# Moving the scaling of half of the value weights from ScalarE to GpSimd at the start of a fused attention and feed-forward block

## What is computed

```
x = x + attn(layernorm(x), Wq, bq, Wk, bk, Wv, bv, Wbeta, bbeta, Walpha, balpha)
x = x + ffn(layernorm(x), gate/up/down weights as 4-bit codes with scales)

attn:  q = (x @ Wq + bq);  k = (x @ Wk + bk);  v = (x @ Wv + bv)
       k = k / norm(k);  alpha = sigmoid(x @ Walpha + balpha);  beta = softplus(x @ Wbeta + bbeta)
       chunks of 128 tokens, 4 heads of 128, decay from cumsum(log(alpha)), state from chunk to chunk
```

## Time and profile before

| what | value |
|---|---|
| median of 3 runs | 1118.35 us (1118.31 to 1118.68) |
| the profiled execution, its own time | 1118.82 us |
| its span in the profile | 1117.1 us |
| TensorE busy | 1106.8 us (99%) |
| VectorE busy | 864.5 us (77%) |
| GpSimd busy | 652.0 us (58%) |
| ScalarE busy | 504.9 us (45%) |

### The profile page before, as it was taken

One profiled execution on the slowest core, in us unless ns is written; L12 is line 12 of the kernel. 1 busy time (PEld: TensorE's weight loads), 2 busy tenths in 40 slices (PEclk: granted clock), 3 DMA queues, 4 the chain that ended last, 5 costly groups with the idle time before them and its releaser, 6 DMA issues.

```text
span 1117.1 us, 22523 instructions
## 1 busy us (share of the span) xinstructions
PE 1106.8 (99%) x8898; PEld 861.3 (77%) x8898; DVE 864.5 (77%) x1516; ACT 504.9 (45%) x1170; POOL 652.0 (58%) x665
## 2 busy tenths in 40 slices
PE   9999999999999899999999999999999999999999
PEld 5656655566457677788888888888888888888886
DVE  7788767468777766688988898889888888886664
ACT  4432345365244344444554455445444544454432
POOL 3376545236783856656775677567756775676330
PEclk9999999999999999999999999999999999999999
DMA  8021111000112223222323232323232323221222
GB/s 305 7 69 47 38 35 42 10 10 1 50 46 76 87 94 114 94 105 104 114 96 106 103 114 95 123 87 114 99 138 78 114 103 123 99 110 77 77 76 76
DMA packets 30233, 96.66 MB, mean 87 GB/s; under 512 B 3440, under 2 KB 3760, under 8 KB 23472
## 3 DMA queue, kind: packets, MB, share of 16 engines
q1 hardware_dynamic: 30128, 95.23, 23.9%
HBM read 63.73 MB, written 31.49 MB: 85 GB/s over the span
## 4 chain that ended last, share of the span: by engine, by line
PE 90%; DVE 3%; POOL 3%; issue 2%; ACT 1%; DMA 0%; SPq 0%; DVEq 0%; POOLq 0%; ACTq 0%
PE ps L649 44%; PE ps L718 19%; PE ps L466 9%; PE ps L758 7%; PE ps L610 6%; PE ps L432 1%; PE ps L552 1%; PE ps L541 1%; PE ps L562 1%; PE ps L476 1%; PE ps L532 0%; PE ps L554 0%; POOL WR L1760 0%; DMA WR<-wqkv 0%; ACT L938 0%
## 5 line engine op out<-in xcount | busy, mean ns | idle before, releaser
L649 PE MATMUL ps<-XT,WR 128*128 128x256 f16 x1344 | 183.3, 273 | 0.0
L649 PE MATMUL ps<-REG,WR 128*128 128x256 f16 x1344 | 183.3, 273 | 0.0
L1059 ACT COPY load<-ps 128x256 f32<-128x256 f32 x168 | 62.4, 371 | 225.7 <-PE ps L649 225.3
L649 PEld LDWEIGHTS ps<-REG,WR 128*128 128x128 f16 x1344 | 130.0, 98 | 21.0
L649 PEld LDWEIGHTS ps<-XT,WR 128*128 128x128 f16 x1344 | 131.5, 98 | 15.4
L1059 ACT COPY bigB<-ps 128x256 f32<-128x256 f32 x168 | 62.5, 372 | 129.5 <-PE ps L649 129.5
L1385 DVE SCALAR_TENSOR_TENSOR X<-ps,X 128x512 f32<-128x512 f32 x161 | 108.0, 683 | 16.2 <-PE ps L718 13.8
L1682 POOL TENSOR_TENSOR ihl_s<-fw,ihl_s 128x512 f16<-128x512 f32 (+1 forms) x46 | 49.5, 1088 | 116.7 <-ACT ihl_s L962 116.7
L1457 DVE TENSOR_TENSOR bigB<-bigB,ps 128x256 f32<-128x256 f32 x168 | 69.5, 414 | 60.2 <-ACT bigB L1059 38.5
L1457 DVE TENSOR_TENSOR load<-load,ps 128x256 f32<-128x256 f32 x168 | 68.7, 413 | 45.3 <-ACT load L1059 31.9
L649 PE MATMUL ps<-REG,bigA 128*128 128x256 f16 x672 | 91.7, 273 | 1.0 <-ACT bigB L1059 1.0
(11 more groups left out here) (244 smaller groups left out, 2536.3 us busy)
## 6 DMA issues: line engine op xcount, KB each, us to landing
kept<-X SPq DMA_DIRECT2D x26, 1024.0 KB, 3.9
X<-kept SPq DMA_DIRECT2D x26, 1024.0 KB, 5.6
load<-codes SPq DMA_DIRECT2D x48, 256.0 KB, 2.7
load<-scales SPq DMA_DIRECT2D x48, 256.0 KB
bigA<-cla SPq DMA_DIRECT2D x14, 256.0 KB, 3.1
X<-x SPq DMA_DIRECT2D x3, 1024.0 KB, 13.3
WR<-wqkv SPq DMA_DIRECT2D x2, 1024.0 KB, 9.9
y<-X SPq DMA_DIRECT2D x2, 1024.0 KB, 4.4
```

What stands on the lines that cost most here:

```text
L649: mm = eng.matmul(half_bank(kind, name), w(wp, kt), x(xp, kt), start=(first and n == 0), stop=(n == 5), skip_group_check=True)
L1059: eng.copy(start, half_bank(kind, name)).then_inc(s_snap, 1)
```

## The change

GpSimd scales and rounds quarters 2 and 3 of the value weights, behind `norm_scale` of block 1, with a semaphore `s_wqp` of its own. ScalarE scales quarters 0 and 1 only, and casts block 0 between them. Whoever waits for a high part (TensorE in both functions, VectorE for the low parts) asks the new function `high`, which gives the semaphore and the count; the counts of the key and query quarters are lower by two.

```
+ON_POOL = (2, 3)
...
+        def high(j, kt):
+            if j == 2:
+                return (s_wqp, kt - 1) if kt in ON_POOL else (s_wqh, kt + 1)
+            return s_wqh, WORDER[j] + kt - 1
...
-                    pe.wait_ge(s_wqh, WORDER[j] + kt + 1)
+                    pe.wait_ge(*high(j, kt))
...
-                            pe.wait_ge(s_wqh, kt + 1)
+                            pe.wait_ge(*high(2, kt))
...
-            weights_high(2, [0, 1])
+            weights_high(2, [0])
             turn("n1", 0)
-            weights_high(2, [2, 3])
+            weights_high(2, [1])
             turn("n1", 1)
             turn("n1", 2)
...
-                    dv.wait_ge(s_wqh, WORDER[j] + k + 1)
+                    dv.wait_ge(*high(j, k))
...
             for T in range(NT):
                 norm_scale("n1", T)
+                if T == 1:
+                    for k in ON_POOL:
+                        pl.wait_ge(s_wv[k], 16)
+                        eng.tensor_scalar(wq[:, 0, k, 1024:1536], wsrc[2][:, k, :], QS, None,
+                                          ALU.mult).then_inc(s_wqp, 1)
```

More of the change, by code:

```diff
@@ L381, in block_kernel @@
             sem(n) for n in ("s_value", "s_vhi", "s_keyw", "s_khi", "s_att", "s_ahi"))
-        s_bvb = sem("s_bvb")
+        s_bvb, s_wqp = sem("s_bvb"), sem("s_wqp")
         s_kw, s_attn, s_dl, s_yl, s_yg = (sem(n) for n in ("s_kw", "s_attn", "s_dl", "s_yl", "s_yg"))
```

## The result

The changed kernel takes 1120.45 us (median of 12 runs, 1119.89 to 1123.38) against 1118.60 for the kernel before in the same session (12 runs). The ratio is 1.0016, with a 95% interval of 1.0009 to 1.0023: slower by 1.85 us (1.0 to 2.6). The forecast was 1118.3 and its range ended at 1119.5. The change is within 0.2% by its middle, but it is slower beyond doubt, and it came out on the side of rival C, the slow scaling.

The account below looks back on a forecast made before the run. TensorE, busy 1106.8 of 1117.1 us, and its early chain of waits bound the kernel. Release at 8.55 instead of 8.61 gave -0.06 us, other parts 0: 1118.76 against the profiled execution, 1118.3 us by the median, range 1117.8 to 1119.5.

Parts of the forecast that it names:

- rival C: GpSimd's two scalings take 1.57 us each, quarter 3 ready at 10.2, TensorE idles 1.6 us more: 1119.9 us; chance 0.14.
- the price of the scaling: GpSimd's 128x512 scalings of quarters 2 and 3: 0.85, then 0.65 us; break-even with ScalarE at 0.80 each.
- the low row: GpSimd's select of line 1650, one operand of 512 elements, 0.64 us at its median, taken as the scaling's price.
- the 0.2 for the first: Added to quarter 2's scaling on GpSimd as a first instruction behind a wait, making it 0.85 us.
- The upper bound: GpSimd's scaling of 512 elements extrapolated from rows of 1, 64 and 128 elements at 2.64 ns an element: 1.57 us.
- The small steps between landing, scalings and TensorE: Only 0.05 us of issue between GpSimd's two scalings was counted; TensorE's extra semaphore wait was costed at nothing.
- one execution's landing of 4.4 us: Quarter 2's transfer, issued at 2.6, was taken to land at 7.0, when GpSimd's first scaling could start.
- the cast of block 0 moves up: On ScalarE the cast starts at 6.7 instead of 7.08, ahead of quarter 1; nothing gained for product 0.
- VectorE wins nothing from it: Low part of block 0 starts 0.3 us earlier, given back waiting for block 2's x at 8.4; costed at nothing.
- the shift is carried whole to 22 us: TensorE's changed release, forecast -0.06 us, passes undiminished through the transposes of block 3 to those of block 4 at 22.17.
- D: Rival: something downstream answers to the shift by more than its size, either way; chance 0.02 on each side.
- TensorE's best gain: Without any wait product 3 could start at 8.27 instead of 8.65, so TensorE can win at most 0.38 us.

Follow-up runs that it names:

- the measurement by itself: Ten extra timed GpSimd instructions (scalings, copy, products) on a tile of ones behind its constants; 1128.83 us in a single run, 10 us above the kernel before.
- the price mended: Changed kernel with a second step, plus 0.0, in GpSimd's two scalings; 1119.08 us against 1119.12 for the kernel before (1.0000).
- the doubled kernel: Changed kernel with each GpSimd scaling made twice, the first time into a tile that nobody reads; 1126.19 us (1.0063 to the kernel before).

## Why the prediction was wrong

- **The step that failed** is the price of the scaling: "I take the low row" (0.64, with 0.2 for the first). It measured 1.51 and 1.50 us, so the 0.2 for the first, behind its wait, was not there either (0.01). The argument for it, that the engine pays for each operand it reads, is right for four forms (0.61, 0.62 and 0.64 with one operand, 1.04 with two) and wrong for the form that the change uses. The upper bound, drawn through three rows of the same opcode, was 1.57: right to 0.06 us. I had two rows of the very form and explained them away as fixed cost that varies. In the code lines 1627 and 1778, of 64 and 128 elements, have `None` for the second step, but line 1620, whose spread of 0.19 to 0.54 was my reason to distrust them, has two steps (add, then mult): it is a row of the other form. The step from 64 to 128 elements was real: 128 elements cost 0.53 in the measurement by itself, 0.557 in the earlier trace rows.
- With 1.5 for 0.65 and 0.85, the prediction's own working gives quarter 3 at 7.0 + 3.0 + 0.05 = 10.05, that is +1.4 and 1119.8. Rival C, at 1.57 each, said 1119.9 and had a chance of 0.14. Measured is +1.85 in the medians.
- **The rest of the gap**, some 0.4 us, has two terms that I had too small. The small steps between landing, scalings and TensorE are 0.21 us where I had 0.05. And I took one execution's landing of 4.4 us as fixed: it is 4.4 to 5.6, and 4.8 in the middle of thirteen profiles, which gives 10.05 + 0.16 + 0.4 = 10.6, +2.0 against the 1.85 measured. That the landings do this in the medians too is inferred from the profiles, not shown, since the timed runs have no trace. The kernel before hides such a landing as long as ScalarE comes to quarter 2 later. The lower clock of one run in twelve does not move the median.
- What held: GpSimd is what TensorE waits for last; the cast of block 0 moves up (to 6.83, where 6.7 was said) and its place is worth nothing (tested, to within 1 us); VectorE wins nothing from it, since block 2's x lands after it (8.99 in the changed kernel); the norm instruction of block 2 is covered by TensorE's own lateness (11.81 against 13.84), as rival C said; the shift is carried whole to 22 us (2.21, 2.21, 2.22). That it changes again behind 60 us, by 0.7 us in this profile, I had given 0.04 in all, as D.
- The forecast of TensorE's best gain, 0.38 us, was never near: with the price mended the release came at 8.95, no earlier than before, as the landing of 4.9 us took up what the lower price won.

## What to carry to other kernels

Price an operation from rows of its own form, its opcode with the same steps, before rows of its size: the one that looked like an outlier was the price. On GpSimd here, a scaling written with a second step that does nothing costs 0.62 us where the one-step form costs 1.49. Where work is moved off the engine that is last, ask what the move exposes besides: here the jitter of a landing that the old order had hidden up to some half a microsecond, and a wait of TensorE long enough to lower its clock.

## What the runs showed of the hardware that was not expected

- GpSimd, 128 x 512 from fp32 to fp16: scaling with no second step 1.49 us, with one 0.62, copy 0.61, product 1.04, whether the second operand is a tile or a repeated column. VectorE's one-step scaling took 0.43.
- The time to landing of the same 256 KB transfer, issued at the same 2.6 us, was 4.4 to 5.6 us in thirteen profiles.
- Two waits of TensorE of 1.1 and 1.2 us with a single product between went with a fall of the clock to 1.2 GHz in one profile (at about 10.9, within the second wait), while it did not fall in another with 0.93 and 1.18. In the doubled kernel, with waits of 2.03 and 2.75, it fell at about 10.5, within the first; with transposes in the waits it did not.
